# Grouped attention: rounded two-part score products, one stream of batches, output product per unit

## What is computed

```python
h = _rms(x, ln_w)
q = (h @ wq).reshape(B, S, 32, 64)
k = (h @ wk).reshape(B, S, 8, 64)
v = (h @ wv).reshape(B, S, 8, 64)
q, k = _rope(q, k)
k, v = jnp.repeat(k, 4, axis=2), jnp.repeat(v, 4, axis=2)
scores = jnp.einsum('bqhd,bkhd->bhqk', q, k) / 8
scores = jnp.where(causal, scores, -1e30)
o = jnp.einsum('bhqk,bkhd->bqhd', softmax(scores), v).reshape(B, S, 2048)
x = x + o @ wo
```

## Time and profile before

| | us |
|---|---|
| median of 3 runs | 3048.33 (3042.65 to 3050.93) |
| the profiled execution | 3039.91 |
| its span, first to last instruction | 3038.1 |
| busy in the span: PE, PEld | 2452.8 (81%), 1662.4 (55%) |
| busy: DVE, ACT, POOL | 1693.3 (56%), 1243.7 (41%), 1324.6 (44%) |
| mean granted clock of TensorE | 0.909 |

### The profile page before, as it was taken

How to read it: one execution, slowest core, us unless ns; L and a number is a source line. 1 busy time by engine, 2 the same in 40 slices (tenths; PEclk the granted TensorE clock), 3 DMA queues, 4 the chain that set the end, 5 groups by cost and what they waited for, 6 DMA issues and landing times. The chain is left out here.

```text
span 3038.1 us, 44303 instructions
## 1 busy us (share of the span) xinstructions
PE 2452.8 (81%) x12088; PEld 1662.4 (55%) x12088; DVE 1693.3 (56%) x5549; ACT 1243.7 (41%) x3486; POOL 1324.6 (44%) x1245
## 2 busy tenths in 40 slices
PE   6999999938998998999899589952657485599992
PEld 6888888934555555556455466531323233277661
DVE  7666666655653662663565343328645656653334
ACT  3444444434542552553454244321445253433331
POOL 3444444414552551553454158862220302117885
PEclk9999999979999999999999789986688796889996
DMA  4000000020000000000000635550000000224554
GB/s 153 15 14 14 14 14 14 5 80 1 1 2 1 2 1 2 1 1 2 1 1 1 227 61 86 86 130 0 1 1 0 0 0 0 112 74 84 86 86 111
DMA packets 72733, 112.48 MB, mean 37 GB/s; under 512 B 11648, under 2 KB 59520, under 8 KB 72128
## 3 DMA queue, kind: packets, MB, share of 16 engines
q0 software_dynamic: 30336, 42.73, 8.7%
q1 hardware_dynamic: 37968, 63.15, 5.9%
q10 hardware_dynamic: 4224, 4.19, 0.4%
HBM read 80.69 MB, written 36.32 MB: 39 GB/s over the span
## 5 line engine op out<-in xcount | busy, mean ns | idle before, releaser
L1017 POOL TENSOR_TENSOR b_sm<-b_sm,b_rden 128x128 f32<-128x128 f32 (+3 forms) x512 | 363.4, 721 | 267.1 <-DVE b_rden L985 257.7
L927 ACT ACTIVATE b_sm<-b_sm,b_mn 128x128 f32<-128x128 f32 (+3 forms) x512 | 286.3, 559 | 349.0 <-DVE b_mn L979 349.0
L848 PEld LDWEIGHTS b_t<-ident,b_sm 128*128 128x128 f32 x1280 | 156.0, 141 | 221.1 <-issue 120.1
L839 PE MATMUL b_s<-b_k,b_q 128*128 128x128 f32 (+3 forms) x688 | 254.1, 454 | 21.8 <-POOL b_q L1004 21.8
L848 PE MATMUL b_t<-ident,b_sm 128*128 128x128 f32 x1280 | 229.7, 278 | 43.3 <-POOL b_sm L1017 30.6
L979 DVE CUSTOM_DVE_ANT_0 b_sm<-b_s,maskB 128x128 f32<-128x128 f32 (+3 forms) x344 | 167.1, 486 | 148.6 <-issue 147.7
L1380 POOL DMA_INDIRECT XN<-rows,m_slots x158 | 158.2, 1001 | 94.0 <-issue 47.6
L409 POOL TENSOR_TENSOR a_q<-a_prod 128x512 f32<-128x512 f32 x64 | 81.8, 1278 | 229.0 <-DVE a_prod L355 229.0
L1962 DVE TENSOR_REDUCE c_nm<-c_first 128x2 f32<-128x1024 f32 x128 | 149.7, 1217 | 35.1 <-PE c_first L1753 35.1
L825 PE MATMUL b_pj<-b_h,b_w 128*128 128x512 f32 x320 | 161.9, 594 | 0.0
L860 PE MATMUL b_o<-b_pt,b_v 128*64 128x512 f32 (+3 forms) x1024 | 157.3, 450 | 3.9 <-DVE b_pt L971 3.9
(11 more groups left out here) (288 smaller groups left out, 5826.7 us busy)
## 6 DMA issues: line engine op xcount, KB each, us to landing
WM<-in_m_w_dram SPq DMA_DIRECT2D x4, 3072.0 KB, 17.0
WM<-in_m_w_dram SPq DMA_DIRECT2D x4, 2432.0 KB, 14.0
acc<-in_zeros_dram SPq DMA_DIRECT2D x3, 2176.0 KB, 15.5
...
XN<-rows,m_slots POOLq DMA_INDIRECT x158, 2.8
...
```

The lines of the kernel that those rows point to most:

```text
L839: pe.matmul(p_s[g % 3][:, 0:keys(t)], q_r[:, m % 2, t * P:(t + 1) * P], kp[:, m // B_REP % 2, head, 0:keys(t)], start=True, stop=True).the ...
L848: x = pe.transpose(p_t[g % 2][:, k * P:(k + 1) * P], sm[:, g % RING, k * P:(k + 1) * P], c.ident[:, :])
L927: act.activation(sm[:, g % RING, 0:keys(t)], sm[:, g % RING, 0:keys(t)], ACT.Exp, scale=-1.0, bias=mn[:, g % RING:g % RING + 1], accum_out ...
L1017: pool.tensor_tensor(sm[:, s, 0:keys(t)], sm[:, s, 0:keys(t)], rden[:, s:s + 1].to_broadcast([P, keys(t)]), ALU.mult).then_inc(s_pn, 1)
```

## The change

It rewrites `attention1`:

- Scores are two products of float32r (rounded) operands into the same bank. The first has the rounded query in the rows of its own head and, copied into the 64 rows that were zero, once more; against it stand the rounded keys and, in the other 64 rows, what rounding left of them. The second has the rest of the query against the rounded, padded keys. The product of the two rests is left out.
- New instructions prepare this: per unit two roundings of 128x512 on ScalarE (`round_q`), two copies of 32x512 on ScalarE and two on VectorE (`double_q`), a subtraction of 128x512 on GpSimd (`low_q`); per four units four copies of 128x512 on ScalarE (`round_k`, in place of `pad`'s two) and four subtractions of 32x512 on VectorE (`low_k`).
- The loops over batches are unrolled into one stream of 64 units. Queries are projected two units ahead; keys and the next batch's values in the items 0 and 1 of units named by `beside`. There is one projection bank (before two), two score banks (before three), and two banks for the output.
- The output product of a unit runs two units later (items 2 and 3) and adds up in the banks; VectorE adds them to XN once a batch. The copy of HT into `h` is gone.

The core of the diff (the functions named above; TensorE's and VectorE's waits and the buffers that the prediction speaks of):

```diff
-    VLAG = CLAG + 1
+    VALUES_AT = CLAG + 1
+    COPY_AT = VALUES_AT + 1
...
+    def beside(M):
+
+        m = M % B_UNITS
+        if M < UNITS and m % B_REP == 1 and M // B_REP + 1 < PAIR_COUNT:
+            return ("k", M // B_REP + 1, 0)
+        if M < UNITS and m in (6, 8, 10, 12) and M // B_UNITS + 1 < BATCH:
+            return ("v", M // B_UNITS + 1, (m - 6) // 2)
+        return None
...
-                    if g == 2:
-                        pe.wait_ge(s_xn, b * TB)
-                    if g >= 3:
-                        pe.wait_ge(s_mn, b * TOTAL + g - 2)
-                    pe.matmul(p_s[g % 3][:, 0:keys(t)], q_r[:, m % 2, t * P:(t + 1) * P],
-                              kp[:, m // B_REP % 2, head, 0:keys(t)], start=True, stop=True).then_inc(s_sc, 1)
...
+                    if G >= 2:
+                        pe.wait_ge(s_mn, G - 1)
+                    out = p_s[G % 2][:, 0:keys(t)]
+                    pe.matmul(out, qh[:, M % 2, head, t * P:(t + 1) * P], k_full[:, pg % 2, head, 0:keys(t)],
+                              start=True, stop=False)
+                    pe.matmul(out, ql[:, M % 2, t * P:(t + 1) * P], k_padded[:, pg % 2, head, 0:keys(t)],
+                              start=False, stop=True).then_inc(s_sc, 1)
...
+                    if G < TOTAL:
+                        scores(G)
+                    if n < 2 and beside(M) is not None:
+                        project(beside(M), n)
+                    if n in (2, 3) and 0 <= M - 2 < UNITS:
+                        out_proj(M - 2, n - 2)
+                    if n in (4, 5) and M + 2 < UNITS:
+                        project(("q", M + 2, 0), n - 4)
+                    if LAG <= G < TOTAL + LAG:
+                        transposes(G - LAG)
+                    if n == VALUES_AT and 0 <= M - 1 < UNITS:
+                        values(M - 1)
...
+                def round_q(M, head):
+
+                    if head == 0:
+                        act.wait_ge(s_rope, ROPES["q", M, 0] + 1)
+                        if M >= 2:
+                            act.wait_ge(s_sc, (M - 1) * ITEMS)
+                    x = act.activation(qh[:, M % 2, head, :], q_r[:, :], ACT.Copy)
+                    if head == 1:
+                        x.then_inc(s_qh, 1)
...
+                    if M + 1 < UNITS:
+                        if n in (1, 2):
+                            round_q(M + 1, n - 1)
+                        if n == 5:
+                            double_q(M + 1)
+                        if M % B_REP == 2 and n in (0, 3) and M // B_REP + 1 < PAIR_COUNT:
+                            round_k(M // B_REP + 1, n // 3)
...
+                def double_q(M):
+
+                    dve.wait_ge(s_qh, M + 1)
+                    for half in range(2):
+                        x = dve.tensor_copy(qh[rows(0, half), M % 2, 1, :], q_r[rows(1, half), :])
+                    x.then_inc(s_qd, 1)
...
+                    if n == 2 and beside(M) is not None:
+                        read(beside(M))
+                    if n in (6, 7) and M + 2 < UNITS:
+                        read(("q", M + 2, 0), n - 6)
+                    if n == 4 and M + 1 < UNITS:
+                        double_q(M + 1)
+                    if M % B_REP == 3 and n in (1, 3) and M // B_REP + 1 < PAIR_COUNT:
+                        low_k(M // B_REP + 1, n // 2)
+                    if n == 5 and M >= 2 and (M - 2) % B_UNITS == B_UNITS - 1:
+                        add_y((M - 2) // B_UNITS)
...
+                    if n == 0 and M + 1 < UNITS:
+                        add(("q", M + 1, 0), q_r)
+                    normalise(G)
+                    if n == 1 and M + 1 < UNITS:
+                        low_q(M + 1)
+                    if n == 2 and beside(M) is not None and beside(M)[0] == "k":
+                        add(beside(M), k_r)
```

More of the change, by code:

```diff
@@ L798, in attention1, with rows, item @@
         s_ov, s_ot, s_y, s_xn = sem("pv"), sem("ot_copied"), sem("out_proj"), sem("added")
[L800 to L805 removed]
+        HALF = B_HD // 2
+        def rows(head, half):
+            lo = half * 2 * HALF + head * HALF
+            return slice(lo, lo + HALF)
+        def item(G):
+            return G // ITEMS, G % 2, (0, 2, 1, 3)[G % ITEMS // 2]
         def keys(t):
@@ L847, in transposes @@
+                def transposes(G):
+                    M, head, t = item(G)
+                    pe.wait_ge(s_pn, G + 1)
+                    if G >= 2:
+                        pe.wait_ge(s_pd if head else s_pa, G // 2)
                     for k in range(t + 1):
-                        x = pe.transpose(p_t[g % 2][:, k * P:(k + 1) * P], sm[:, g % RING, k * P:(k + 1) * P], c.ident[:, :])
+                        x = pe.transpose(p_t[G % 2][:, k * P:(k + 1) * P], sm[:, G % RING, k * P:(k + 1) * P], c.ident[:, :])
@@ new lines, in _ @@
+                pe.wait_ge(s_w, 16 * 6)
+                for job in order[0:TB + 3]:
+                    project(job)
+                for G in range(LAST):
+                    M, n = G // ITEMS, G % ITEMS
+                    if G < TOTAL:
[10 more added lines that the diff above has]
+                        values(M - 1)
@@ new lines, in inverse, with add_y @@
+                def inverse(G):
+                    s = G % RING
+                    dve.wait_ge(s_exp, G + 1)
+                    dve.reciprocal(rden[:, s:s + 1], den[:, s:s + 1]).then_inc(s_rd, 1)
+                def add_y(b):
+                    dve.wait_ge(s_y, (b + 1) * B_UNITS)
+                    for a in range(2):
+                        to = c.XN[:, b * TB + 2 * a:b * TB + 2 * a + 2, :].rearrange("p t d -> p (t d)")
+                        x = dve.tensor_tensor(to, p_y[a][:, :], to, ALU.add)
+                    x.then_inc(s_xn, 1)
@@ new lines, in _ @@
+                dve.wait_ge(s_w, 16 * 6)
+                for job in order[0:TB + 3]:
+                    read(job)
+                    if job[0] == "k":
+                        low_k(0, 0)
+                        low_k(0, 1)
+                    elif job == ("q", 0, 0):
+                        double_q(0)
+                for G in range(LAST):
+                    M, n = G // ITEMS, G % ITEMS
+                    if CLAG <= G < TOTAL + CLAG and item(G - CLAG)[1] == 1:
+                        copy_pt(G - CLAG)
+                    if G < TOTAL:
+                        minimum(G)
+                    if INV <= G < TOTAL + INV:
+                        inverse(G - INV)
+                    if n == 2 and beside(M) is not None:
[8 more added lines that the diff above has]
+                        add_y((M - 2) // B_UNITS)
@@ new lines, in _ @@
+                add(("k", 0, 0), k_r)
+                add(("q", 0, 0), q_r)
+                low_q(0)
+                for G in range(TOTAL):
+                    M, n = G // ITEMS, G % ITEMS
+                    if n == 0 and M + 1 < UNITS:
[5 more added lines that the diff above has]
+                        add(beside(M), k_r)
```

360 lines of the change are left out of this document (171 added, 189 removed).

## The result

| | before | after |
|---|---|---|
| median of 20 runs each, us | 3044.96 (3040.46 to 3050.93) | 3050.07 (3045.1 to 3057.38) |
| ratio, 95% interval | | 1.0018 [1.0009, 1.0026] |
| span of the profiled execution, us | 3038.1 | 3043.5 |
| stage, to the last addition to XN, us | 1013.7 | 1019.5 |
| stream: first score to last score, us | | 977.1 |

The account below looks back on a forecast made before the run. A loop through TensorE, VectorE, GpSimd and ScalarE was taken to bound the attention unit: 13.9 + 0.17 + 0.15 + 0.35 + 0.25 = 14.8 us. With head and tail the stage took 985 against 1013.7, giving 3019 us, range 2935 to 3085.

Parts of the forecast that it names:

- rival 5: Whole kernel: gains and losses cancel within 9 us, no effect; chance 0.08.
- the loop: One attention unit: score, minimum, query read, GpSimd's normalisations and add, ScalarE's rounding, then TensorE; period 13.9 us.
- The plain loop: Attention unit where nothing else is late: 9.4 us up to TensorE's transpose plus 4.5 of TensorE, 13.9.
- copies: VectorE's new copies of 32 rows beside GpSimd's subtraction: between 0 and 0.75 us a unit, taken as 0.35.
- Units with a projection beside: In 8 of 16 units TensorE waits for the query read through the single bank: 14.25 us, plus 0.35 / 2 = 0.17.
- Keys rounded: ScalarE rounds keys ahead of item 4's exponential in 4 of 16 units: plus 0.6 / 4 = 0.15 us.
- low keys: VectorE's subtractions in 4 of 16 units: 0 to 2.2 us, taken as 1.0 / 4 = 0.25.
- rival 4: VectorE and GpSimd conflicts at double the size: unit 15.7 us, stage 1042, program 3076; chance 0.10.
- Head and tail: Attention stage before its first score and after its last: head 31 us where 21 stood, tail 14.
- Rival 3: TensorE's waits lower its clock, 1.2 GHz for 14% of the time: 0.9 us a unit, 3076 us; chance 0.16.
- Rivals 1 and 2: The first: no conflict of copies and GpSimd, period 14.2, 2982 us, chance 0.20; for the second see Rival 2.
- Rival 2: ScalarE's wait is not on the path, TensorE and VectorE alone close the loop: 13.2 a unit, 2919 us; chance 0.12.

Follow-up runs that it names:

- e1: Changed kernel with GpSimd adding the rotated query ahead of item 6 of the unit before, instead of behind item 7: 3027.2 us, 0.9951.
- e2: Changed kernel with VectorE doing both parts of the query read at item 6, instead of the second behind item 7's minimum: 2943.5 us, 0.9668.
- e3: Changed kernel with both moves, those of e1 and e2, together: 2904.9 us, 0.9542.
- e6: Changed kernel without VectorE's two copies of 32 rows (`double_q`): 1.0016.
- e10: Changed kernel with a buffer of its own for the key's two products: 1.0014.
- e14: Kernel of e13 with the key's own product buffer of e10: 3024.4 us, 0.9934.
- e13: Changed kernel with five additional rounded products, overwritten by the score behind them, in TensorE's long wait: 0.9982.
- e4: Changed stream with one float32 product for a score, as before, and without roundings, doublings and low parts: 3084.1 us, 1.0133.
- e9: Kernel of e1 with five additional rounded products in TensorE's long wait, ahead of item 0 in units with a projection beside, else item 1: 2990.0 us, 0.9819.
- e15: Kernel of e4 with two additional float32 products of 384 columns in TensorE's long wait: 1.0011.

## Why the prediction missed

It named 3019, faster with chance 0.63, and 5 us slower was measured: rival 5, no effect, which had 0.08. The result lies in the range. By its own steps:

- **What bounds the kernel, and the loop**: right. The marks of the mechanism are there: ScalarE idle before the first rounding until GpSimd's add (115.5 us in all), TensorE's transpose ahead of item 5's score released by ScalarE's copy, and the two waits of TensorE. One mark was not seen as named: the score that waits for a minimum (19 times, 0.19 to 0.3 us) is item 1's, for the minimum of item 7, not one for item 0's. The marks of size say wrong: the period is 15.39, over the 15.3 named as the end of the forecast, the clock 0.94, not 0.97, and subtraction and normalisation rows are longer than 1.27 and 1.04 (1.30, 1.09). e1 and e2 opened the loop at the two named places, and e3 moved the mean period (of products with the values) from 15.27 to 13.04.
- **The plain loop, 13.9**: with the copies' 0.35, 14.25 was forecast and 14.5 came. In the unit shown above the minimum starts 0.91 after the score and not 0.66, and GpSimd could start at 4.07, not 3.65; from its add to TensorE's transpose it is 2.4, as summed; TensorE's rest took 4.9, not 4.5. None of the small misses is on the other side. e6, without the copies, has 14.26, so the loop itself is nearly 0.4 over and the copies 0.1 under. A chain of a dozen rows summed from start to start needs a reserve at the handoffs; here it was 0.3 a unit, 3 us over the 11 plain ones.
- **"Units with a projection beside, plus 0.35"**: the step that failed. It followed TensorE's single bank up to the query's read, and did not follow the key's own read, which waits for GpSimd's add through the shared buffer of products, and on which the next query's projection waits. 1.4 over the forecast in 15 units is **21 us**, the largest part of the miss. Of the 1.4, 0.8 is shown to be this buffer (e10, e14), 0.3 is what the plain unit is over as well, and for the last 0.3 the cause is open. For values the term of 0.35 was 0.04.
- **Keys rounded, 0.15; low keys, 0.25; copies, 0.35**: the unit with keys rounded is right to 0.03 us, but by luck: the term measured 0.37 (14.88 - 14.51) where 0.6 was taken, and that made up for the plain loop's miss. The low keys measured 1.04 in their unit where 1.0 was taken, though the unit as a whole is 0.3 over like the plain one; the copies 0.17 and not 0.35. The conflict goes both ways, which the prediction tied to its upper bounds; it came at a fraction of rival 4's price.
- **Head and tail**: 29.3 + 13.1 for 31 + 14, 2 to 3 us better.
- **Rival 3, the clock**: given 0.16, with the place right (two waits of 1.8 and 1.3, measured 1.74 and 1.07), the amount nearly right (14% of the time at 1.2 GHz forecast, 113 of 962 us, 12%, measured) and the price wrong: it charged the whole 0.9 us a unit as if TensorE bounded the unit, and e13 measured 11 us, 0.2 a unit. It is a part of the miss, not the other side. Where TensorE is nearer the path, in e1 and e4, it is 40 and 37 us, the 0.6 of a unit.
- **The sum**: 3 (plain) + 4 (low keys, 15 units at 0.3) + 21 (key) + 11 (clock) is 39, and 37 were measured in the 63 periods; the last units are short, which makes up about 1. Less the 2 to 3 of head and tail this is 35, which is the distance from 29 forecast to 6 lost.

Rivals 1 and 2 did not occur. Rival 2's number was too low for its own condition: e1 takes just ScalarE's wait away, and with the clock held (e9) its mean period is 14.3 and its time 2990, not 13.2 and 2919. That e3 comes near it (2905) is chance, since e3 moves the query's read too.

## What to carry to other kernels

When items become a stream, the order in which each engine takes its once-a-unit work sets the period: look for the engine that waits for a late step of another (an add behind two normalisations, a read behind the last minimum) and move that step by one item before judging the change. Follow every buffer that two jobs share, not only the bank: here a key's read hung behind the query's add. And where TensorE idles 1.7 us or more in one piece in such a stream, look for half clock behind it; shorten that one wait, or fill it, before saving smaller times elsewhere, since they may come back as nothing (e10) until it is done.

## What the runs showed of the chip

- Single idle pieces of 1.7 to 1.9 us, in a stream where TensorE is busy 0.83 to 0.88 of the time, are followed in part of the cases by some 3 us at clock 0.50 (33 of 62 in the changed kernel); with the longest idle piece cut down by other products there was none (e9, e13, e15: 0 us). The busy share does not tell them apart: from 900 to 1100 us e4 is busy 0.89 with clock 0.97, e13 0.88 with clock 1.00. How short a piece is harmless isn't settled: 26 pieces of 1.07 to 1.13 had nothing behind them in e13, and three of 1.07 or 1.08 had a stretch at half clock behind them in e3.
- Added products made a kernel faster: e9 0.9819 against 0.9951.
- Of equal time at half clock, 113 and 106 us, 11 us reach the end in one order and 40 in another.
- VectorE's passes over 32 rows with source and target in SBUF stretch GpSimd's neighbouring instructions by 0.05 to 0.1 us in the mean (827 to 928, 1040 to 1094), and a pair of them beside two normalisations took 2.79.
